# Sums by block in a graph layer: half a spot made a unit sooner, stores begun by POOL, early sums added by a diagonal product

## The reference

```python
h0 = relu(layernorm(x))
h, q, k, v = h0 @ Wn + bn, h0 @ Wq + bq, h0 @ Wk + bk, h0 @ Wv + bv
hmid = leaky(concat([q[src], k[dst], edge @ We + be]) @ A1 + b1)
w = softmax(mean(leaky(hmid @ A2 + b2), heads), over all edges)
out = segment_sum(w * v[dst], src, 12500)
y = h + out
return x + gamma * (y - mean(y)) / sqrt(var(y) + 1e-5) + beta
```

## Time and profile before

| what | value |
|---|---|
| runs | 5091.33, 5094.11, 5094.43 us; median 5094.11 |
| the profiled execution | 5090.77 us, span 5089.0 us |
| mean granted TensorE clock | 0.962 |
| busy share of the whole span | PE 88%, DVE 78%, POOL 63%, ACT 55% |
| the sums by block | from about 4583 to 5083 us |

### The profile page before, as it was taken

One profiled execution on the slowest core, in us unless ns is written; L12 is line 12 of the kernel. 1 busy time (PEld: TensorE's weight loads), 2 busy tenths in 40 slices (PEclk: granted clock), 3 DMA queues, 4 the chain that ended last, 5 costly groups with the idle time before them and its releaser, 6 DMA issues. The chain is left out here.

```text
span 5089.0 us, 137207 instructions
## 1 busy us (share of the span) xinstructions
PE 4457.4 (88%) x35287; PEld 3598.7 (71%) x35287; DVE 3988.6 (78%) x9656; ACT 2813.0 (55%) x7064; POOL 3194.0 (63%) x3381
## 2 busy tenths in 40 slices
PE   8665567888899999999999999999999986997887
PEld 3544455666688878788788878887887764776776
DVE  7655556767788888888888888888888774768998
ACT  5333333444466666666666666665666542436666
POOL 2677777777777777777777777777777772000010
PEclk9888888999999999999999999999999998999999
DMA  8888877988999988988898888988888766888887
GB/s 248 196 237 258 252 232 242 271 265 259 280 317 317 317 256 258 262 261 254 262 266 262 257 256 263 263 265 250 264 263 261 224 186 176 220 230 211 227 231 211
DMA packets 1938630, 1276.12 MB, mean 251 GB/s; under 512 B 637802, under 2 KB 1830929, under 8 KB 1938444
## 3 DMA queue, kind: packets, MB, share of 16 engines
q1 hardware_dynamic: 1768101, 831.59, 62.7%
q0 software_dynamic: 154752, 435.99, 23.1%
q10 hardware_dynamic: 15592, 6.41, 0.5%
HBM read 703.28 MB, written 570.23 MB: 250 GB/s over the span
## 5 line engine op out<-in xcount | busy, mean ns | idle before, releaser
L1266 POOL DMA_INDIRECT slots<-rows,slot_i x3224 | 3104.1, 963 | 992.4 <-issue 916.9
L1321 PE MATMUL ps_row<-win,mixed 128*128 128x256 f32 x5904 | 1530.2, 405 | 115.8 <-ACT rows L1410 109.9
L1321 PEld LDWEIGHTS ps_row<-win,mixed 128*128 128x128 f32 x5904 | 1112.0, 200 | 299.3 <-ACT rows L1410 134.7
L1410 ACT ACTIVATE rows<-ps_row 128x512 f32<-128x512 f32 x1476 | 890.3, 603 | 52.5 <-PE ps_row L1321 49.7
L1407 ACT ACTIVATE rows<-lo_all 128x8 f32 (+1 forms) x403 | 87.3, 217 | 1452.2 <-DMA slots<-rows,slot_i 1452.0
L1292 PE MATMUL ps_e<-ident,edges 128*128 128x128 f32 x3224 | 511.5, 283 | 259.6 <-ACT mixed L1399 172.8
L1292 PEld LDWEIGHTS ps_e<-ident,edges 128*128 128x128 f32 x3224 | 417.0, 147 | 425.5 <-ACT mixed L1399 180.2
L773 PE MATMUL ps_z<-onehot,q_bits 128*128 128x512 bf16 (+1 forms) x2646 | 700.5, 374 | 0.2 <-DVE onehot L856 0.2
L844 ACT ACTIVATE low<-ps_z 128x512 f32<-128x512 f32 (+1 forms) x882 | 528.2, 599 | 309.1 <-PE ps_lo L757 165.6
L866 DVE TENSOR_TENSOR mid<-low,ps_z 128x512 f32<-128x512 f32 (+1 forms) x882 | 588.6, 667 | 130.0 <-ACT low L844 104.5
L1463 ACT ACTIVATE early_v<-early_v,early_weight 128x128 f32<-128x128 f32 x1960 | 600.0, 415 | 0.0
(11 more groups left out here) (217 smaller groups left out, 5713.8 us busy)
## 6 DMA issues: line engine op xcount, KB each, us to landing
u_rows<-slots SPq DMA_DIRECT2D x880, 258.0 KB, 3.2
early_v<-slots SPq DMA_DIRECT2D x490, 258.0 KB
edges<-edge_attr_dram SPq DMA_DIRECT2D x403, 256.0 KB
q_bits<-qb_tab SPq DMA_DIRECT2D x882, 96.0 KB, 3.1
slots<-no_row SPq DMA_DIRECT2D x98, 528.0 KB
slots<-rows,slot_i POOLq DMA_INDIRECT x3224
v_own<-slots SPq DMA_DIRECT2D x198, 258.0 KB, 3.3
slots<-no_row SPq DMA_DIRECT2D x98, 396.0 KB
```

The source lines that it names most:

```text
L1266: pool.indirect_dma_start(slots_tab[h], bass.IndirectOffsetOnAxis(slot_i[:, u, j:j + 1], 0), rows[:, u, j, :], None).then_inc(scattered[u] ...
L1321: last = pe.matmul(bank[:, j % 2, :], mixed[:, u % 2, j, :], win[:, u, :], start=True, stop=True)
L1410: nc.scalar.activation(rows[:, u, 2 * k:2 * k + 2, 0:2 * U0].rearrange("p j (a c) -> p j a c", a=2)[:, :, :, 0:D], row_bank(s, k).rearrang ...
```

## The change

`KEPT = PRELOADED - 1`: 55 blocks' part_in are taken from the preloaded ones, block 55 loads its own. `y_chain` counts five operations a block. The sums' core:

```diff
 # SP
-                        if not preloaded(i, all_wide):
-                            sp.dma_start(part_in[:, bass.ds(t - PRELOADED, 1), :], nodes_of(h_tab, t, 1)).then_inc(xr_in[b], 16)
+                        if not preloaded(t, all_wide):
+                            sp.dma_start(part_in[:, bass.ds(t - KEPT, 1), :], nodes_of(h_tab, t, 1)).then_inc(xr_in[b], 16)
...
 # POOL
+                def store_block(t, b, all_wide):
+
+                    pool.wait_ge(o_ready, t + 1)
+                    pool.sem_inc(passed, 1)
+                    for p0, p1 in ((0, SPLIT), (SPLIT, P if wide(t, all_wide) else P - 1)):
+                        pool.dma_start(rows_of_block(out, t, p0, p1), o_sb[p0:p1, b, :]).then_inc(o_out[b], 16)
+
+                def block_step(i, k, all_wide):
+
+                    add_beta(i, k, all_wide)
+                    if k % LATE == LATE - 1 and has(i, k) and past(i, k - LATE):
+                        store_block(i * BLOCKS + (k // LATE - 1), (k // LATE - 1) % 2, all_wide)
...
-                    unit_steps(pool, add_beta)
+                    unit_steps(pool, block_step)
+                    store_block(NT - 1, (NT - 1) % 2, False)
+                    pool.wait_ge(o_out[0], 32 * (NT // 2))
+                    pool.wait_ge(o_out[1], 32 * (NT // 2))
...
 # PE
-                    if k % LATE == 0 and past(i, k - 2 * LATE):
-                        pe.wait_ge(y_chain, i * (6 * BLOCKS) + (6 * (k // LATE) - 10))
+                    if k % LATE == 0:
+                        if past(i, k - 2 * LATE):
+                            pe.wait_ge(y_chain, i * (5 * BLOCKS) + (5 * (k // LATE) - 9))
+                        if known(i) and i == 0 and k == 0:
+                            pe.wait_ge(scale_ready, 1)
+                        t = i * BLOCKS + k // LATE
+                        pe.matmul(ps_y[:, b, 0:D], part_scale[:], acc_sb[:, bass.ds(t, 1), :].rearrange("p a k -> p (a k)"),
+                                  start=True, stop=False, skip_group_check=True)
                     for c in range(rows_at(k)):
                         last = pe.matmul(ps_y[:, b, 0:D], spot[:, k % SPOTS, c, :], v_rows(k % VRING)[:, c, 0:D],
-                                         start=(k % LATE == 0 and c == 0), stop=(k % LATE == LATE - 1 and c == SHORT - 1),
+                                         start=False, stop=(k % LATE == LATE - 1 and c == SHORT - 1),
...
 # ACT (its store_block and store are gone)
-                def place_last(i, k):
+                def part_last(i, k):
 
                     g, c = i * PAIR + k, rows_at(k) - 1
                     act.wait_ge(v_in[k % VRING], ring_count(i, k, VRING) + v_before[k % VRING])
+                    if past(i, k - 2):
+                        act.wait_ge(last_ready, g - 1)
                     nc.scalar.activation(apart[:, k % 2, :], iota_f[:], ACT.Abs, scale=-1.0,
                                          bias=v_rows(k % VRING)[:, c, D:D + 1]).then_inc(apart_ready, 1)
+
+                def place_last(i, k):
+
+                    g, c = i * PAIR + k, rows_at(k) - 1
                     if first_of_bunch(k) and past(i, k - SPOTS):
                         act.wait_ge(y_part, bunches(i, k - SPOTS))
                     act.wait_ge(apart_ready, g + 1)
...
                 def sum_step(i, k, all_wide):
+                    if has(i, k + LEAD + 1):
+                        part_last(*unit_at(i, k + LEAD + 1))
                     if has(i, k + LEAD):
                         place_last(*unit_at(i, k + LEAD))
...
 # DVE (add_part and the product part_inv * inv are gone)
                     if part_of == 1:
                         dve.wait_ge(y_part, (t + 1) * BUNCHES[-1])
-                        dve.wait_ge(y_chain, t * 6 + 1)
+                        dve.wait_ge(xb_ready, t + 1)
...
                         nc.vector.scalar_tensor_tensor(y_sb[:], ps_y[:, b, 0:D], inv[:, 0:1],
-                                                       acc_sb[:, bass.ds(t, 1), :].rearrange("p a k -> p (a k)"),
+                                                       part_in[:, bass.ds(here, 1), :].rearrange("p a k -> p (a k)"),
...
+                def scale_parts():
+
+                    nc.vector.tensor_scalar(part_scale[:], ident[:], part_inv[:, 0:1], None, ALU.mult).then_inc(scale_ready, 1)
```

More of the change, by code:

```diff
@@ L1845, in unit_steps, with preloaded @@
             one_pair(SUMS_END)
-        def preloaded(i, all_wide):
-            return i < PRELOADED // BLOCKS if known(i) else all_wide
+        KEPT = PRELOADED - 1
+        def preloaded(t, all_wide):
+            return t < KEPT if known(t) else all_wide
         assert PRELOADED // BLOCKS == FULL_BODIES + 1 and PRELOADED % (2 * BLOCKS) == 0 and NT - PRELOADED <= PRELOADED
@@ L1952, in gnn_layer @@
         y_std_ready = sem("y_std_ready")
+        scale_ready = sem("scale_ready")
         xb_ready = sem("xb_ready")
@@ L2383, in root @@
                     t = i * BLOCKS + (k // LATE - 1)
-                    act.wait_ge(y_chain, t * 6 + 4)
+                    act.wait_ge(y_chain, t * 5 + 3)
                     nc.scalar.activation(y_std[:], y_mv[:, 1:2], ACT.Sqrt, bias=eps[:, 0:1]).then_inc(y_std_ready, 1)
[L2387 to L2396, removed]
                 def part_of(table, n, passes):
@@ L2410, in negate_weights @@
                     nc.scalar.mul(part_of(minus, n, LATE), part_of(weight, n, PASSES)[:, SOONER:PASSES, :], -1.0).then_inc(minus_ready, 1)
+                def part_last(i, k):
+                    g, c = i * PAIR + k, rows_at(k) - 1
+                    act.wait_ge(v_in[k % VRING], ring_count(i, k, VRING) + v_before[k % VRING])
+                    if past(i, k - 2):
+                        act.wait_ge(last_ready, g - 1)
+                    nc.scalar.activation(apart[:, k % 2, :], iota_f[:], ACT.Abs, scale=-1.0,
+                                         bias=v_rows(k % VRING)[:, c, D:D + 1]).then_inc(apart_ready, 1)
                 def place_last(i, k):
                     g, c = i * PAIR + k, rows_at(k) - 1
-                    act.wait_ge(v_in[k % VRING], ring_count(i, k, VRING) + v_before[k % VRING])
-                    nc.scalar.activation(apart[:, k % 2, :], iota_f[:], ACT.Abs, scale=-1.0,
-                                         bias=v_rows(k % VRING)[:, c, D:D + 1]).then_inc(apart_ready, 1)
                     if first_of_bunch(k) and past(i, k - SPOTS):
@@ L2434, in sum_step @@
                         root(i, k)
-                        store(i, k, all_wide)
                 def with_slots():
@@ L2448, in with_slots @@
                     act.wait_ge(minus_ready, 1)
+                    part_last(0, 0)
                     for k in range(LEAD):
+                        part_last(0, k + 1)
                         place_last(0, k)
@@ L2580, in place @@
                     op.then_inc(spot_ready, 1)
-                def add_part(t, i, all_wide):
-                    dve.wait_ge(xb_ready, t + 1)
-                    if known(t) and t == 0:
-                        dve.wait_ge(parts_in, 16 * -(-PRELOADED // 8))
-                    here = t if preloaded(i, all_wide) else t - PRELOADED
-                    of_block = acc_sb[:, bass.ds(t, 1), :].rearrange("p a k -> p (a k)")
-                    nc.vector.scalar_tensor_tensor(of_block, of_block, part_inv[:, 1:2],
-                                                   part_in[:, bass.ds(here, 1), :].rearrange("p a k -> p (a k)"), ALU.mult, ALU.add
-                                                   ).then_inc(y_chain, 1)
@@ L2593, in finish @@
-                def finish(t, b, part_of):
+                def finish(t, b, part_of, all_wide):
                     if part_of == 1:
                         dve.wait_ge(y_part, (t + 1) * BUNCHES[-1])
-                        dve.wait_ge(y_chain, t * 6 + 1)
+                        dve.wait_ge(xb_ready, t + 1)
+                        if known(t) and t == 0:
+                            dve.wait_ge(parts_in, 16 * -(-PRELOADED // 8))
+                        here = t if preloaded(t, all_wide) else t - KEPT
@@ L2637, in sum_step @@
                         for part_of in ((), (1, 2), (3,), (4, 5))[k % LATE]:
-                            finish(i * BLOCKS + (k // LATE - 1), (k // LATE - 1) % 2, part_of)
-                    if k % LATE == LATE - 1 and has(i, k):
-                        add_part(i * BLOCKS + k // LATE, i, all_wide)
+                            finish(i * BLOCKS + (k // LATE - 1), (k // LATE - 1) % 2, part_of, all_wide)
                 def with_slots():
@@ L2654, in with_slots @@
                     dve.wait_ge(exp_ready, 1)
+                    scale_parts()
                     for k in range(LEAD):
```

24 lines of the change are left out of this document (10 added, 14 removed).

## The result

The changed kernel took **5123.2 us** (median of 5 runs, 5121.92 to 5125.17) against 5094.11 for the kernel before: 1.0062 times, 95% interval 1.0052 to 1.0073. It is slower, inside the range, 14 us above the time named. The profiled execution has a span of 5121.6 us against 5089.0: 32.6 us to be found.

What follows compares the result with a forecast made beforehand. DVE was taken to bound the sums at 4.95 us a block, with the ring of loads a second limit. Ring +6 and +9.5 and end 1.7 made +17, named as 5109 us; the range went from 5069 to 5135.

Steps and rivals of the forecast that it cites:

- rival (b): Sums by block: two stores at 1.9 to 2.3 cancel DVE's gain; 5082 to 5100 us, hardly any change; chance 0.20.
- sign of being wrong: Sums by block: POOL's two stores delay xb by less than 1.9 us, or values land soon enough that nothing waits.
- DVE alone: Sums by block: DVE loses acc_sb, 0.26 a block, and alone would need 4.69 instead of 4.95, 25 us over 96 blocks.
- PE and ACT: Sums by block: PE at 4.53 and ACT at 4.3 us a block stay under DVE's 4.69 and cost nothing.
- The ring: Sums by block, output through xb and loads to next output: 7.6 plus stores 2.53, 10.13 per two blocks, +6 and +9.5 us.
- the price of POOL's two stores: POOL, between output and xb: 2.53 us, from indirect DMAs at 1.27 each; range 0.8 to 3.0.
- the load of part_in: Sums from block 55 on: this load between output and first value adds 0.22 to the ring.
- a ring of 9.6: Sums by block: the skill page's estimate, two stores at 2.0 us, giving a time of some 5085 us.
- rival (a): Sums by block: stores under 1.8 us, DVE stays the bound at 4.69 a block; 5067 to 5070 us; chance 0.30.
- Rival (c): Sums by block: DVE and POOL get in each other's way, +42 or +74 us; price 5135 to 5170; chance 0.14.
- At the start: Start: scale_parts adds about 0.26 on DVE, an inversion product of like size goes; all covered, zero cost.
- The end: After the last output: the last store leaves POOL 1.7 us later, 2.53 - 0.82.

Runs made afterwards that it cites:

- e4: The changed kernel, but POOL stores block t-2 right behind making xb of block t, instead of t-1 ahead of xb of t+1; 0.9934 times the kernel before.
- e9: The changed kernel with POOL storing the 49 odd blocks and ACT the 49 even ones; 1.0063 times the kernel before.
- e11: The changed kernel with the stores of finished blocks and the waits at the end back on ACT; 5062.0 us, 0.9940 times the kernel before.
- The fourth job: The last group of follow-up runs, on a slower chip: e12 with the kernel before beside it; ratio 0.9994.
- e2: The kernel before with one part of the change alone, POOL storing finished blocks and waiting for them at the end; 1.0006 times the kernel before.
- e5: The changed kernel itself, run again on a chip with a slower first stage; 1.0025 times the kernel before.
- e7: The changed kernel with the last block's store and the wait for it on ACT, the 97 others on POOL; 1.0016 times the kernel before.
- e10: The changed kernel with ACT, not POOL, waiting at the end for the stores' landing; 1.0059 times the kernel before.
- e12: e4 with its stores raising two semaphores of the first stage's indirect DMAs instead of two of their own; 0.9994 times the kernel before.

## Why the prediction came out as it did

**The sign was right by luck: no step of the forecast had its reason.** The forecast was slower by a longer ring: +6 and +9.5 in the sums, +1.7 behind. Measured: 2.9 less in the sums, 6.2 more behind, and 29.3 ahead of them. Without the last, which nothing in the profile of before foretold, the time would have been some 5094, within 0.2% of before. In the sums it is rival (b), balance, that came true: 4.82 early, where (b) had 4.75 to 4.95. The forecast's own sign of being wrong came too: the stores delay xb by 1.8 us, less than 1.9. DVE busy down to 88 (88.29 on average from 4700 to 5100) and waits on the values' DMAs once a block did show; outputs 5.07 apart, two DMAs near 1.27 each and 2.5 us more of SP's wait a block did not. That wait could not grow so: a block takes no longer than before, and SP comes to the wait later, since its earlier loads were held back too.

- **DVE alone.** 4.69 a block was worked out from 4.95 - 0.26. With the stores off POOL it is 4.65 to 4.67 early and, without the last four blocks, 4.72 late: right, and the gain is 29.7 us instead of 25.
- **PE and ACT.** PE at 4.53 was to be no bound; e4 goes to 4.62 with PE busy for 93.31 of 100 us, and DVE for 95.05 (6320 to 6420). ACT was put at 1.08 a unit; in the timeline above it goes from apart to spot in 0.31 and from spot to apart in 0.54, so 0.85, and no row has apart waiting for a spot, as was named. Neither held anything but by waiting for values.
- **The ring** was the right mechanism, and e4 and e9 show it. The step that was mis-sized is the price of POOL's two stores, 2.53. They take 1.11 busy (540 ns the median of one), and begin 1.08 to 1.16 after the output where xb began after 0.43. Together they put 1.8 into the ring. The legs of the turn shown are 2.28, 0.83, 1.07, 3.03, 0.12 until DVE uses the value, and 2.53 to the output: 9.86. The legs read in the earlier trace rows come to 7.3 without the stores, so the stores have 1.85 of it and the others 0.7 more than was read. On average an early turn is 9.64 (4.82 a block), and 7.6 + 1.8 would have been 9.4. In the late blocks it is 10.18, 0.54 more where 0.22 were expected (the pause of POOL told of below and the short last blocks are in this average and about cancel). That is the load of part_in. The forecast took its price from one turn of the earlier trace rows, 2.43 from output to first value, and that turn was untypical: in the kernel before, the turns from 4960 to 5057 have 2.77 to 2.91, as in this one (2.90):

```profile
5021.83 0.35 DVE L2617 SCALAR_TENSOR_TENSOR o_sb<-y_g,y_rstd,xb 128x128 f32<-128x128 f32 x1
...
5023.06 0.89 SPq L2118 DMA_DIRECT2D x_rows<-x_dram  x2
5024.16 0.37 SPq L2120 DMA_DIRECT2D part_in<-h_tab  x1
5024.73 2.40 SPq L2110 DMA_DIRECT2D v_own<-slots  x4
```

In the changed kernel output to first value is 3.96 to 4.21 early and 4.57 to 4.64 late, 0.56 more on average:

```profile
5038.89 0.35 DVE L2630 SCALAR_TENSOR_TENSOR o_sb<-y_g,y_rstd,xb 128x128 f32<-128x128 f32 x1
...
5041.81 0.88 SPq L2122 DMA_DIRECT2D x_rows<-x_dram  x2
...
5042.91 0.37 SPq L2124 DMA_DIRECT2D part_in<-h_tab  x1
...
5043.47 0.39 SPq L2114 DMA_DIRECT2D v_own<-slots  x1
```

The Trainium skill, DMA: Bandwidth & Descriptors (Latency and other measured facts), had given, as an estimate by its 1 us, a ring of 9.6: nearer than the row of another kind of DMA, though as a sum of other parts (0.65 of a later start and 1.1 of issue).

- **So rival (a) and the forecast met in the middle, which is (b)**: DVE's gain of 29.7 us less the 26.8 by which the changed kernel's sums are longer than e11's left 2.9. Of the 26.8 some 2.9 are the one pause of POOL told of below, which no step had. (a) gave the stores up to 1.8 before the ring decides; they took just that, and it decided.
- **Rival (c), contention**, is out for this stage: spots last 348 ns on average beside POOL's stores, 344 before.
- **At the start** all was held to be covered, and so it was: the first output follows the last indirect DMA by 365.4 us as before (365.3). What was wrong was to take the first stage as untouched because its code is.
- **The end** was priced by the stores' issue alone, +1.7. It is +6.2, and the term that was missing is POOL's ending behind its last work, which follows the last store now that POOL has it.

## What to carry to other kernels

When an engine gets its first work of a new kind, look at everything that engine does in the whole program, the stages that the change doesn't touch too: 9 ns on 3224 instructions cost 29 us here, as much as the change gained on DVE. When a leg is priced from one turn of a loop, look at a few more turns first: the late load cost 0.56, not 0.22. Before a step is put into an engine's order, ask which wait of a loop stands behind it: the same stores on the same engine cost 33 us more ahead of xb than behind it. And an engine that ends last brings its own ending with it; give the last work to one that ends quickly.

## What was not expected of the hardware

- Plain DMAs in POOL's program, even one pair that runs at the very end, raised the indirect DMAs from a median of 960 ns to 969 to 972, and their minimum from 954 or 956 to between 963 and 967: nine profiles of eight kernels with such DMAs, five profiles of two kernels without. The fourth job has no profile of a kernel without them. New semaphores aren't the cause (970 with old ones).
- Behind POOL's last store it took from 5.3 us (one pair in all) to 12.8 until the span ended.
- A plain store of 112 or 16 rows costs POOL 540 ns of issue, an indirect one of 128 rows 960. ACT's pair costs 0.82, POOL's 1.11, but POOL's begins 0.65 us later behind the same wait than its own vector operation does.
- Once in each profile in which POOL stores 97 or 98 blocks ahead of xb (changed, e2, e5, e7, e10), POOL pauses behind xb of about block 64 for 6.2 to 6.8 us with no wait shown (the row "POOL out_dram <- issue" above; in the changed kernel from 4941.5), and four blocks then take 23.3 instead of 20.4 us. In e4 and e12, with the stores behind xb, the pause is 3.2 and costs 0.3 or less; e9, with half the stores on POOL, has none. Its cause was not looked for.
